# Layer 3 attention: a mixing laid out as two heads by two query halves, turned before the next scores

## The chip, the cores and the metric

The kernel runs on one core of one Trainium2 chip. The metric is the device time of one execution in microseconds, the median of the runs. The engines are named as the profile names them: PE multiplies matrices (PEld loads its stationary operands), DVE, ACT and POOL work on vectors, SP issues DMAs.

## The reference

The whole kernel is a decoder of four layers, each with an attention, a cross attention and a feed-forward block, on 16 times 128 = 2048 tokens of width 256. The change touches the attention of layer 3 alone:

```python
proj = jnp.einsum('bsd,ed->bse', x, proj_w) + proj_b
flat = jnp.transpose(proj.reshape(B, S, H, hd), (2, 0, 1, 3)).reshape(H, B * S, hd)
q = jnp.einsum('hnd,hde->hne', flat, wq)
k = jnp.einsum('hnd,hde->hne', flat, wk)
logits = jnp.einsum('hne,hme->hnm', q, k) / jnp.sqrt(jnp.asarray(D, x.dtype))
attn = jax.nn.softmax(logits, axis=-1)
out = jnp.einsum('hnm,hmd->hnd', attn, flat)
```

There are H = 16 heads of hd = 16, and all 2048 tokens attend to all 2048 in every head. The result is added to x.

## The kernel before, in words

`l3_attn` (from L4443) first projects and splits queries and keys into parts (phase "split"), and then runs the phase "heads", which is all that the change touches. It works in 32 units: eight pairs of heads by four chunks of 512 queries. A unit has 32 steps, sixteen tiles of 128 keys by two heads. The steps of all units are one sequence, `steps`, which every engine's program walks in the same order, starting 48 steps early (`LEAD`).

Each even step n has, in PE's own order (L4757 to L4771):

- two probes (L4727), queries against 512 keys, one per head of a pair. They run one unit and a half ahead and serve only to find each query's largest score; DVE takes the maximum of both in one reduction (L4783).
- `score(n)` (L4717), 128 keys by 512 queries of the first head, into one of three PSUM banks that rotate (`slot_of`, `SB` = 3). The row maxima are part of the operands, so ACT only has to take the exponential (L4820) into one of 16 `attn` tiles.
- half of `mix` (L4742), attention times values, for the scores of 8 steps ago. The values have 17 columns, 16 and a column of ones that gives the softmax sum, padded to 32. Four such strips stand side by side on the array: two heads by two key tiles. `mix(m, 0)` and `mix(m, 1)` do the two halves of 256 query columns.
- `score(n + 1)`, the second head. Both heads' operands have 50 rows, on different halves of the array (rows 0 to 49 and 64 to 113).

Each strip's product of one half is two recorded matmuls, so a half of `mix` shows eight. The strips add up in PSUM bank 7 (`mixed_bank`) over the unit's sixteen key tiles: 512 columns, and per head two partial sums, for even and odd key tiles.

When a unit has ended, its result is taken out during the next unit, at fixed steps (`ended_at`, L4658):

- step 6: ACT copies bank 7 to `output` (`out`, L4831, 128x512). The next unit's first `mix`, at step 8, waits for this copy (`outed`, L4738 to L4740), since it overwrites the bank.
- step 15, behind `score(15)`: PE turns `output` by four 128x128 transposes (`unturn`, L4752) into one of the three rotating banks; ACT copies that to `unturned` (`take`, L4837, 128x512), behind `exp(15)`.
- step 17: POOL adds the even and the odd partial sums (`add_halves`, L4893).
- step 24: DVE takes the reciprocal of the sums (`divide`, L4800); POOL multiplies (L4899) and adds to x (L4903).

POOL also rounds and lays the maxima into the queries for the unit after (`lay_rows`, L4885), and SP loads the next pair's operands.

Of the kernel before, what the change touches and what calls it, by code (L numbers as in the profile page):

```python
# [13 lines left out]
ALU = mybir.AluOpType  # L14
# [3 lines left out]
P = 128  # L18
# [7 lines left out]
PAD = 32  # L26
# [4416 lines left out]
def l3_attn(k):  # L4443
# [15 lines left out]
    with ExitStack() as stack:  # L4459
# [172 lines left out]
                    pool.wait_ge(s["lined"], 4)  # L4632

        RING, SPAN, LEAD = 16, 2 * QT, 48
        SB, PB = 3, 4
        UNITS = PAIRS * CHUNKS
        TOTAL = UNITS * SPAN
# [2 lines left out]
        peaks = sb(k, stack, "peaks", [P, 2, 4, 2, CHUNKS])  # L4640
        peak = sb(k, stack, "peak", [P, 2, 4, 2])
        peak_parts, peak_rows = (sb(k, stack, m, [P, 2, 4, 2, PAD]) for m in ("peak_parts", "peak_rows"))
        output = sb(k, stack, "output", [P, CHUNK])
        unturned = sb(k, stack, "unturned", [P, 4, 4, PAD])
        sums, fresh = sb(k, stack, "sums", [P, 4, 2, VW]), sb(k, stack, "fresh", [P, 4, 2, D])
        share = sb(k, stack, "share", [P, 4, 2])
        mixed_bank = k.ps[:, 7, :]
        steps = range(-LEAD, TOTAL + SPAN)
        OUT, UNTURN, SUM, DIVIDE, TURN, RAISE = 6, 15, 17, 24, 5, 8

        def scored(n):
            return 0 <= n < TOTAL
# [8 lines left out]

        slot_of = {}
        for n_ in steps:
            jobs = [("score", n_)] if scored(n_) else []
            if ended_at(n_, UNTURN) is not None:
                jobs.append(("unturn", ended_at(n_, UNTURN)))
            for job in jobs:
                slot_of[job] = len(slot_of)

        def bank(job):  # L4670
            return k.ps[:, slot_of[job] % SB, :]

        names = ("loaded0 loaded1 pool_step cleared fetched probed maxed peaked parted rows_turned raised scored read mixed outed "
                 "unturned summed shared added value_made value_took biased")
        with phase(k, "heads", names) as (block, s):
            loaded = [s[f"loaded{i}"] for i in range(2)]

# [15 lines left out]
            def _(pe):  # L4693
# [36 lines left out]
                        last.then_inc(s["probed"], 1)  # L4730

                def mix(m, half):
                    u, part = m // 8, m % 8
                    columns = sl(half, CHUNK // 2)
                    if half == 0:
                        pe.wait_ge(s["read"], slot_of["score", 4 * m + 3] + 1)
                    if part == 0 and half == 0:
                        pe.wait_ge(s["fetched"], u // CHUNKS + 1)  # L4738
                        if u >= 1:
                            pe.wait_ge(s["outed"], u)  # L4740
                    for strip in range(4):
                        last = nc.tensor.matmul(mixed_bank[sl(strip, PAD), columns], head_values[:, u // CHUNKS % 2, strip % 2, 2 * part + strip // 2, :],  # L4742
                                                attn[:, (4 * m + strip) % RING, columns], start=part == 0 and half == 0, stop=part == 7 and half == 1,
                                                skip_group_check=True)
                    if half == 1:
                        last.then_inc(s["mixed"], 1)

                def unturn(u):
                    pe.wait_ge(s["outed"], u + 1)
                    slot_free(("unturn", u))  # L4750
                    for b in range(4):
                        last = nc.tensor.transpose(bank(("unturn", u))[:, sl(b)], output[:, sl(b)], k.ident[:, :])  # L4752
                    last.then_inc(s["unturned"], 1)

# [2 lines left out]
                for n in steps:  # L4757
                    if n < 16 - LEAD and n % 4 == 0:
                        value(4 + (n + LEAD) // 4)
                    if n % 2 == 0:  # L4760
                        for p in (n + LEAD, n + LEAD + 1):
                            if p < TOTAL:
                                probe(p)
                        if scored(n):
                            score(n)
                        if scored(4 * (n // 4 - 2)):
                            mix(n // 4 - 2, n % 4 // 2)
                        if scored(n + 1):
                            score(n + 1)
                    if ended_at(n, UNTURN) is not None:  # L4770
                        unturn(ended_at(n, UNTURN))  # L4771

            @block.vector
            def _(dve):
                v = nc.vector
                v.memset(head_values[:, :, :, :, :], 0.0).then_inc(s["cleared"], 1)

                def peak_of(p):
                    r, i, at = p // SPAN, p % SPAN // 2, SB + p % PB
                    if i == 0 and r >= 2:  # L4780
                        dve.wait_ge(s["peaked"], r - 1)
                    dve.wait_ge(s["probed"], p // 2 + 1)
                    v.tensor_reduce(peaks[:, r % 2, i // CHUNKS, :, i % CHUNKS], k.ps[:, at:at + 2, :], AX.X, ALU.max).then_inc(s["maxed"], 1)  # L4783

                def peak_of_all(r):
                    dve.wait_ge(s["maxed"], 16 * (r + 1))
                    if r >= 2:
                        dve.wait_ge(s["parted"], r - 1)
                    v.tensor_reduce(peak[:, r % 2, :, :], peaks[:, r % 2, :, :, :], AX.X, ALU.max, negate=True).then_inc(s["peaked"], 1)  # L4789

                def turn_rows(r):
                    dve.wait_ge(s["parted"], r + 1)
                    if r >= 2:
                        dve.wait_ge(s["raised"], 8 * (r - 1))
                    v.transpose(peak_rows[:, r % 2, :, :, :].rearrange("p b a c -> p (b a c)"),  # L4795
                                peak_parts[:, r % 2, :, :, :].rearrange("p b a c -> p (b a c)")).then_inc(s["rows_turned"], 1)

                def divide(u):
                    dve.wait_ge(s["summed"], u + 1)
                    v.reciprocal(share[:, :, :].unsqueeze(3), sums[:, :, :, D:VW]).then_inc(s["shared"], 1)  # L4800

                for n in steps:
                    p = n + LEAD
                    if p < TOTAL:
                        if p % 2:
                            peak_of(p - 1)
                        if p % SPAN == SPAN - 1:
                            peak_of_all(p // SPAN)
                    if row_at(n, TURN) is not None:
                        turn_rows(row_at(n, TURN))  # L4810
                    if ended_at(n, DIVIDE) is not None:
                        divide(ended_at(n, DIVIDE))

            @block.scalar
            def _(act):
# [17 lines left out]
                def take(u):  # L4833
                    act.wait_ge(s["unturned"], u + 1)
                    if u >= 1:
                        act.wait_ge(s["summed"], u)
                    nc.scalar.activation(unturned[:, :, :, :].rearrange("p b a w -> p (b a w)"), bank(("unturn", u)),  # L4837
                                         ACT.Copy).then_inc(s["read"], 1)

                for i in range(QT // 2):  # L4840
                    take_values(i)
                for n in steps:
                    if scored(n):
                        exp(n)
                    if ended_at(n, OUT) is not None:
                        out(ended_at(n, OUT))
                    if ended_at(n, UNTURN) is not None:
                        take(ended_at(n, UNTURN))

            @block.gpsimd  # L4850
            def _(pool):
                link = Link(pool, s["pool_step"])
                g_ = nc.gpsimd
                done = {"fetched": 0, "parted": 0, "summed": 0, "added": 0}

                def fetch(pair):
                    if pair == 0:
# [27 lines left out]
                            g_.tensor_copy(rows[:, :, quarter, :], peak_rows[PAD * quarter:PAD * quarter + 2, r % 2, :, a, :]).then_inc(s["raised"], 1)  # L4885
                    pool.wait_ge(s["raised"], 8 * (r + 1))

                def add_halves(u):
                    pool.wait_ge(s["read"], slot_of["unturn", u] + 1)
                    if u >= 1:  # L4890
                        pool.wait_ge(s["shared"], u)
                        pool.wait_ge(s["added"], 2 * u)
                    g_.tensor_tensor(sums[:, :, :, :], unturned[:, :, 0:2, 0:VW], unturned[:, :, 2:4, 0:VW], ALU.add).then_inc(s["summed"], 1)  # L4893
                    done["summed"] += 1

                def add(u):
                    pair, c = u // CHUNKS, u % CHUNKS
                    pool.wait_ge(s["shared"], u + 1)
                    g_.tensor_tensor(fresh[:, :, :, :], sums[:, :, :, 0:D], share[:, :, :].unsqueeze(3).broadcast_to([P, 4, 2, D]),  # L4899
                                     ALU.mult).then_inc(s["added"], 1)  # L4900
                    pool.wait_ge(s["added"], 2 * u + 1)
                    x = k.x[:, sl(c, 4), sl(pair, 2 * D)].rearrange("p b (a d) -> p b a d", a=2)
                    g_.tensor_tensor(x, x, fresh[:, :, :, :], ALU.add).then_inc(s["added"], 1)  # L4903
                    done["added"] += 2

                def add_bias(i):
# [11 lines left out]
                for n in steps:  # L4918
# [3 lines left out]
                        lay_rows(row_at(n, RAISE))  # L4922
                    if n > 0 and n % (CHUNKS * SPAN) == CHUNKS * SPAN - 16 and n // (CHUNKS * SPAN) + 1 < PAIRS:
                        fetch(n // (CHUNKS * SPAN) + 1)
                    if ended_at(n, SUM) is not None:
                        add_halves(ended_at(n, SUM))
                    if ended_at(n, DIVIDE) is not None:
                        add(ended_at(n, DIVIDE))

# [222 lines left out]
```

## Time and profile before

| | us |
|---|---|
| runs | 3328.42, 3354.23, 3327.92 |
| median | 3328.42 |
| span of the profiled execution, first to last instruction | 3397.0 |
| of it, phase "heads": first probe to the end of the last addition to x | 2429.4 to 3148.1 |

The profile knows no other time of that execution than its span. Times inside it are counted from the span's start.

### The profile page before, as it was taken

What the parts mean: (1) busy time and instruction counts of PE and PEld (TensorE: products, weight loads), DVE (VectorE), ACT (ScalarE), POOL (GpSimd) and SP (SyncE); (2) the same over time, 40 slices, a digit from 0 to 9 for tenths busy, and PEclk for the clock granted to TensorE, in tenths of its full rate; (3) what the DMA queues carried; (4) which work ended last, traced back from release to release, by engine and by line L of the source; (5) the groups of instructions that cost most, each with busy time, mean ns of one, the idle gap of its engine ahead of it and who ended that gap; (6) DMA issues with size and microseconds to landing.
All of it is one profiled execution on the core that took longest, in us unless ns stands there. A gap on an engine that the chain in (4) does not pass through costs nothing. (4 is left out here: it accounts for less than half of the span.)

```text
span 3397.0 us, 59298 instructions
## 1 busy us (share of the span) xinstructions
PE 3009.1 (89%) x20925; PEld 1857.6 (55%) x20929; DVE 2235.3 (66%) x4489; ACT 1822.0 (54%) x4182; POOL 1132.7 (33%) x1288
## 2 busy tenths in 40 slices
PE   7979759998887799987799989797799999999889
PEld 4656548877664556653467657454333333333567
DVE  6777645454546656667567747525589999996672
ACT  6967713333213344445566645211278888888554
POOL 3535555433432022215166653012111111221333
PEclk9999869999998999998889999898789999999989
DMA  9300156665530000022000032132401111110300
GB/s 301 133 9 2 47 203 210 207 188 173 158 101 26 26 1 1 1 73 85 33 1 1 1 118 106 64 109 88 113 1 20 20 21 20 21 20 1 125 13 25
DMA packets 158228, 243.61 MB, mean 72 GB/s; under 512 B 21298, under 2 KB 130482, under 8 KB 152482
## 3 DMA queue, kind: packets, MB, share of 16 engines
q1 hardware_dynamic: 144114, 202.05, 19.6%
q0 software_dynamic: 13824, 37.77, 3.4%
q8 instruction: 173, 2.83, 0.4%
q14 instruction: 117, 0.96, 0.1%
HBM read 132.64 MB, written 107.10 MB: 71 GB/s over the span
## 5 line engine op out<-in xcount | busy, mean ns | idle before, releaser
L4783 DVE TENSOR_REDUCE peaks<-ps 128x2 f32<-128x1024 f32 x512 | 617.6, 1219 | 64.8 <-PE ps L4727 63.0
L4820 ACT ACTIVATE attn<-ps 128x512 f32<-128x512 f32 x1024 | 558.8, 596 | 113.1 <-PE ps L4717 56.8
L4717 PE MATMUL ps<-queries,keys 50*128 50x512 f32 x1024 | 383.8, 455 | 0.0
L4727 PE MATMUL ps<-keys,queries 50*128 50x512 f32 x1024 | 370.2, 468 | 12.8 <-DVE peaks L4783 7.9
L4742 PE MATMUL ps<-attn,head_values 128*32 128x256 f32 x4096 | 332.3, 397 | 9.2 <-ACT output L4831 9.2
L4717 PEld LDWEIGHTS ps<-queries,keys 50*128 50x128 f32 x1024 | 157.6, 188 | 215.6 <-ACT attn L4820 197.5
L1239 POOL TENSOR_TENSOR attn_w<-attn_w,attn_share 128x512 f32<-128x512 f32 x128 | 131.7, 1050 | 373.0 <-DVE attn_share L1085 373.0
L2133 PE MATMUL ps<-experts,tileT 128*128 x884 | 232.0, 385 | 2.1 <-issue 2.1
L2340 DVE COPY normed<-ps 128x256 f32<-128x256 f32 x221 | 93.8, 424 | 202.9 <-PE ps L2149 106.8
L4742 PEld LDWEIGHTS ps<-attn,head_values 128*32 128x32 f32 x4096 | 82.3, 108 | 197.9 <-issue 108.6
L2194 ACT ACTIVATE tileT<-ps 128x256 f32<-128x256 f32 x221 | 84.6, 383 | 168.4 <-PE ps L2117 115.7
L2149 PE MATMUL ps<-experts,hiddenT 128*128 (+1 forms) x474 | 147.2, 392 | 25.1 <-DVE hiddenT L2349 21.1
L2133 PEld LDWEIGHTS ps<-experts,tileT 128*128 128x128 f32 x884 | 153.2, 193 | 19.4 <-issue 3.8
L4727 PEld LDWEIGHTS ps<-keys,queries 50*128 50x128 f32 x1024 | 147.5, 192 | 28.4 <-DVE peaks L4783 16.6
L2200 ACT ACTIVATE gate<-ps 128x128 f32<-128x128 f32 x237 | 65.8, 277 | 173.9 <-PE ps L2133 152.6
L1076 DVE TENSOR_REDUCE attn_peak<-ps 128x4 f32<-128x512 f32 x128 | 87.7, 685 | 95.9 <-PE ps L958 95.9
L4870 POOL CAST peak_parts<-peak 128x8 fp32r<-128x8 f32 x32 | 6.3, 197 | 407.4 <-DVE peak L4789 387.8
L2050 POOL DMA_INDIRECT rows<-expert_rows,index x96 | 91.0, 948 | 150.2 <-DMA expert_rows<-normed 60.9
L972 PE MATMUL ps<-xT,L_xattn_Wq 128*128 128x512 f32 x256 | 124.7, 610 | 7.7 <-ACT qT L1176 6.2
L2038 POOL DMA_INDIRECT routed_rows<-rows,index x96 | 96.3, 1003 | 87.7 <-DVE normed L2340 61.5
L2149 PEld LDWEIGHTS ps<-experts,hiddenT 128*128 128x128 f32 x474 | 86.8, 191 | 52.8 <-issue 41.1
L4885 POOL CAST queries<-peak_rows 2x128 fp32r<-2x128 f32 x256 | 73.5, 287 | 125.3 <-DVE peak_rows L4795 111.6
(733 smaller groups left out, 7164.5 us busy)
## 6 DMA issues: line engine op xcount, KB each, us to landing
tile_in<-routed_rows SPq DMA_DIRECT2D x244, 128.0 KB, 2.2
expert_rows<-normed SPq DMA_DIRECT2D x221, 128.0 KB
routed_rows<-zeros SPq DMA_DIRECT2D x2, 8064.0 KB, 48.1
experts<-in_L_ffn_experts SPq DMA_DIRECT2D x4, 3072.0 KB
routed_rows<-zeros SPq DMA_DIRECT2D x1, 12160.0 KB, 67.0
kT<-L_xattn_keys SPq DMA_DIRECT2D x8, 1024.0 KB
v<-L_xattn_values SPq DMA_DIRECT2D x8, 1024.0 KB, 8.7
experts<-in_L_ffn_experts SPq DMA_DIRECT2D x8, 1024.0 KB
```

Of the source, the lines that this page charges most:

```text
L972: last = nc.tensor.matmul(query_bank, wq[:, kt, sl(4 * p + jj)], xT[g % 2][:, kt, :], start=kt == 0, stop=kt == KD - 1)
L1239: nc.gpsimd.tensor_tensor(w, w, share[:, n % 2, side, :].unsqueeze(2).broadcast_to([P, 4, P]), ALU.mult).then_inc(s_["scaled"], 1)
L2038: nc.gpsimd.indirect_dma_start(rows_dram[g][:, :], bass.IndirectOffsetOnAxis(index_of(slice(t, t + 1))[:, 0, c:c + 1], 0), rows[:, t, :], ...
L2050: nc.gpsimd.indirect_dma_start(rows[:, TOP * (t % 2) + c, :], None, back_dram[g][:, :], bass.IndirectOffsetOnAxis(index[:, t, c:c + 1], 0) ...
L2133: last = nc.tensor.matmul(gate_bank(u), x, weight(u, 2 * kt * INNER, 2 * INNER), start=False, stop=kt == KD - 1)
L2149: nc.tensor.matmul(out_bank(u), hiddenT[:, u % 2, :], weight(u, 2 * KD * INNER, DIM), start=is_tile(u), stop=True).then_inc(s["downed"], 1)
L2340: v.tensor_copy(tile_out[:, u % 4, :], out_bank(u)).then_inc(s["out_taken"], 1)
L4717: nc.tensor.matmul(bank(("score", n)), keys[pair % 2][rows, sl(kt)], queries[pair % 2][rows, sl(c, CHUNK)], start=True, stop=True).then_in ...
L4727: last = nc.tensor.matmul(k.ps[:, SB + p % PB, :], queries[pair % 2][rows, sl(t)], keys[pair % 2][rows, sl(c, CHUNK)], start=True, stop=True)
L4742: last = nc.tensor.matmul(mixed_bank[sl(strip, PAD), columns], head_values[:, u // CHUNKS % 2, strip % 2, 2 * part + strip // 2, :], attn[ ...
L4783: v.tensor_reduce(peaks[:, r % 2, i // CHUNKS, :, i % CHUNKS], k.ps[:, at:at + 2, :], AX.X, ALU.max).then_inc(s["maxed"], 1)
L4820: nc.scalar.activation(attn[:, n % RING, :], bank(("score", n)), ACT.Exp, scale=1.0 / 16.0).then_inc(s["read"], 1)
```

## The change

The four strips of `mix` become two heads by two halves of the query columns. `mix(m, half)` now does one key tile for all 512 queries, where it did two key tiles for half of them: `block` is the key tile, `side` the query half. So no strip is a partial sum, the result is 256 columns instead of 512, and `add_halves` with its semaphore goes. `out` and `take` copy 256 columns, `unturn` has two transposes. POOL's last addition is two instructions of half the size, as the blocks now lie two tiles apart in x.

`unturn` moves from behind `score(15)` to in front of it, directly behind the `mix` of step 14; its bank stands before that of `score(15)` in the rotation, and ACT's `take` moves in front of `exp(15)`. `mix` waits for its exponentials in both halves, each time for the two tiles that it reads. `divide`, `take` and `add` wait for other semaphores in place of the removed one.

```diff
@@ -4632,6 +4632,7 @@
         RING, SPAN, LEAD = 16, 2 * QT, 48
+        HALF = CHUNK // 2
         SB, PB = 3, 4
@@ -4640,13 +4641,12 @@
-        output = sb(k, stack, "output", [P, CHUNK])
-        unturned = sb(k, stack, "unturned", [P, 4, 4, PAD])
-        sums, fresh = sb(k, stack, "sums", [P, 4, 2, VW]), sb(k, stack, "fresh", [P, 4, 2, D])
-        share = sb(k, stack, "share", [P, 4, 2])
-        mixed_bank = k.ps[:, 7, :]
+        output = sb(k, stack, "output", [P, HALF])
+        unturned, fresh = sb(k, stack, "unturned", [P, 2, 4, PAD]), sb(k, stack, "fresh", [P, 2, 4, D])
+        share = sb(k, stack, "share", [P, 2, 4])
+        mixed_bank = k.ps[:, 7, 0:HALF]
         steps = range(-LEAD, TOTAL + SPAN)
-        OUT, UNTURN, SUM, DIVIDE, TURN, RAISE = 6, 15, 17, 24, 5, 8
+        OUT, UNTURN, DIVIDE, TURN, RAISE = 6, 15, 24, 5, 8
@@ -4661,9 +4661,9 @@
-            jobs = [("score", n_)] if scored(n_) else []
-            if ended_at(n_, UNTURN) is not None:
-                jobs.append(("unturn", ended_at(n_, UNTURN)))
+            jobs = [("unturn", ended_at(n_, UNTURN))] if ended_at(n_, UNTURN) is not None else []
+            if scored(n_):
+                jobs.append(("score", n_))
@@ -4730,17 +4730,16 @@
                 def mix(m, half):
-                    u, part = m // 8, m % 8
-                    columns = sl(half, CHUNK // 2)
-                    if half == 0:
-                        pe.wait_ge(s["read"], slot_of["score", 4 * m + 3] + 1)
-                    if part == 0 and half == 0:
+                    u, block = m // 8, 2 * (m % 8) + half
+                    pe.wait_ge(s["read"], slot_of["score", 4 * m + 2 * half + 1] + 1)
+                    if block == 0:
                         pe.wait_ge(s["fetched"], u // CHUNKS + 1)
                         if u >= 1:
                             pe.wait_ge(s["outed"], u)
                     for strip in range(4):
-                        last = nc.tensor.matmul(mixed_bank[sl(strip, PAD), columns], head_values[:, u // CHUNKS % 2, strip % 2, 2 * part + strip // 2, :],
-                                                attn[:, (4 * m + strip) % RING, columns], start=part == 0 and half == 0, stop=part == 7 and half == 1,
+                        side, a = strip // 2, strip % 2
+                        last = nc.tensor.matmul(mixed_bank[sl(strip, PAD), :], head_values[:, u // CHUNKS % 2, a, block, :],
+                                                attn[:, (4 * m + 2 * half + a) % RING, sl(side, HALF)], start=block == 0, stop=block == QT - 1,
                                                 skip_group_check=True)
@@ -4748,7 +4747,7 @@
                 def unturn(u):
-                    for b in range(4):
+                    for b in range(2):
@@ -4765,10 +4764,10 @@
                             mix(n // 4 - 2, n % 4 // 2)
+                        if ended_at(n + 1, UNTURN) is not None:
+                            unturn(ended_at(n + 1, UNTURN))
                         if scored(n + 1):
                             score(n + 1)
-                    if ended_at(n, UNTURN) is not None:
-                        unturn(ended_at(n, UNTURN))
@@ -4796,8 +4795,10 @@
                 def divide(u):
-                    dve.wait_ge(s["summed"], u + 1)
-                    v.reciprocal(share[:, :, :].unsqueeze(3), sums[:, :, :, D:VW]).then_inc(s["shared"], 1)
+                    dve.wait_ge(s["read"], slot_of["unturn", u] + 1)
+                    if u >= 1:
+                        dve.wait_ge(s["added"], 2 * u)
+                    v.reciprocal(share[:, :, :].unsqueeze(3), unturned[:, :, :, D:VW]).then_inc(s["shared"], 1)
@@ -4833,25 +4834,25 @@
                 def take(u):
                     act.wait_ge(s["unturned"], u + 1)
                     if u >= 1:
-                        act.wait_ge(s["summed"], u)
-                    nc.scalar.activation(unturned[:, :, :, :].rearrange("p b a w -> p (b a w)"), bank(("unturn", u)),
+                        act.wait_ge(s["added"], 2 * u)
+                    nc.scalar.activation(unturned[:, :, :, :].rearrange("p b c w -> p (b c w)"), bank(("unturn", u))[:, 0:HALF],
                                          ACT.Copy).then_inc(s["read"], 1)
                 for n in steps:
+                    if ended_at(n, UNTURN) is not None:
+                        take(ended_at(n, UNTURN))
                     if scored(n):
                         exp(n)
                     if ended_at(n, OUT) is not None:
                         out(ended_at(n, OUT))
-                    if ended_at(n, UNTURN) is not None:
-                        take(ended_at(n, UNTURN))
@@ -4885,22 +4886,18 @@
-                def add_halves(u):
...
-                    g_.tensor_tensor(sums[:, :, :, :], unturned[:, :, 0:2, 0:VW], unturned[:, :, 2:4, 0:VW], ALU.add).then_inc(s["summed"], 1)
...
                 def add(u):
                     pair, c = u // CHUNKS, u % CHUNKS
                     pool.wait_ge(s["shared"], u + 1)
-                    g_.tensor_tensor(fresh[:, :, :, :], sums[:, :, :, 0:D], share[:, :, :].unsqueeze(3).broadcast_to([P, 4, 2, D]),
+                    if u >= 1:
+                        pool.wait_ge(s["added"], 2 * u)
+                    g_.tensor_tensor(fresh[:, :, :, :], unturned[:, :, :, 0:D], share[:, :, :].unsqueeze(3).broadcast_to([P, 2, 4, D]),
                                      ALU.mult).then_inc(s["added"], 1)
                     pool.wait_ge(s["added"], 2 * u + 1)
-                    x = k.x[:, sl(c, 4), sl(pair, 2 * D)].rearrange("p b (a d) -> p b a d", a=2)
-                    g_.tensor_tensor(x, x, fresh[:, :, :, :], ALU.add).then_inc(s["added"], 1)
+                    for b in range(2):
+                        x = k.x[:, 4 * c + b:4 * c + b + 3:2, sl(pair, 2 * D)].rearrange("p s (a d) -> p s a d", a=2)
+                        last = g_.tensor_tensor(x, x, fresh[:, b, :, :].rearrange("p (s a) d -> p s a d", s=2), ALU.add)
+                    last.then_inc(s["added"], 1)
@@ -4922,8 +4919,6 @@
-                    if ended_at(n, SUM) is not None:
-                        add_halves(ended_at(n, SUM))
```

## Rows read from the trace of the kernel before

**Rows 1.** The page, its head and part 1: busy us, share, instructions.

```profile
span 3397.0 us, 59298 instructions
...
PE 3009.1 (89%) x20925; PEld 1857.6 (55%) x20929; DVE 2235.3 (66%) x4489; ACT 1822.0 (54%) x4182; POOL 1132.7 (33%) x1288
```

**Rows 2.** Busy time by stretch: stretch, length, PE, PEld, DVE, ACT, POOL, clock, DMA.

```profile
2661.00:2761.00 100.00, 98.57 (x932) 37.53 (x930) 93.74 (x91) 87.53 (x162) 17.81 (x57) 1.00 0.12 17
...
2707.77:2728.86 21.09, 20.80 (x198) 7.91 (x198) 19.82 (x20) 18.45 (x36) 4.61 (x14) 1.00 0.20 33
```

**Rows 3.** Waits, 2480 to 3110 us: waiter, released by, us, times, longest.

```profile
DVE peaks L4783 <- PE ps L4727: 40.3, 94, 1.0
...
PE ps L4742 <- ACT output L4831: 8.6, 30, 0.3
```

**Rows 4.** Timeline of PE, steps 5 to 9: start, busy us, instruction.

```profile
2706.27 0.50 PE L4717 MATMUL ps<-queries,keys 50*128 50x512 f32 x1
...
2706.93 0.64 PE L4742 MATMUL ps<-attn,head_values 128*32 128x256 f32 x8
...
2707.50 0.50 PE L4717 MATMUL ps<-queries,keys 50*128 50x512 f32 x1
...
2707.84 0.39 PE L4717 MATMUL ps<-queries,keys 50*128 50x512 f32 x1
...
2708.52 0.64 PE L4742 MATMUL ps<-attn,head_values 128*32 128x256 f32 x8 [0.29 <-ACT output L4831]
...
2709.09 0.49 PE L4717 MATMUL ps<-queries,keys 50*128 50x512 f32 x1
```

**Rows 5.** Timeline of PE, the mixing of step 14 to step 17.

```profile
2712.22 0.64 PE L4742 MATMUL ps<-attn,head_values 128*32 128x256 f32 x8
...
2712.79 0.49 PE L4717 MATMUL ps<-queries,keys 50*128 50x512 f32 x1
...
2713.21 0.66 PE L4752 MATMUL ps<-ident,output 128*128 128x128 f32 x4
...
2713.79 0.50 PE L4727 MATMUL ps<-keys,queries 50*128 50x512 f32 x2
...
2714.45 0.64 PE L4742 MATMUL ps<-attn,head_values 128*32 128x256 f32 x8
...
2715.02 0.49 PE L4717 MATMUL ps<-queries,keys 50*128 50x512 f32 x1
```

**Rows 6.** Timeline of PE, the first three of those four transposes.

```profile
2713.21 0.55 PE L4752 MATMUL ps<-ident,output 128*128 128x128 f32 x3
```

**Rows 7.** Timeline of ACT over the same steps.

```profile
2707.77 0.60 ACT L4831 ACTIVATE output<-ps 128x512 f32<-128x512 f32 x1
...
2708.25 1.11 ACT L4820 ACTIVATE attn<-ps 128x512 f32<-128x512 f32 x2
...
2713.90 0.60 ACT L4837 ACTIVATE unturned<-ps 128x512 f32<-128x512 f32 x1
```

**Rows 8.** The page, part 5: ACT copying 256 columns out of PSUM.

```profile
L2194 ACT ACTIVATE tileT<-ps 128x256 f32<-128x256 f32 x221 | 84.6, 383 | 168.4 <-PE ps L2117 115.7
```

**Rows 9.** Timeline of DVE: after the transposes, and three reductions after a delay.

```profile
2714.41 1.23 DVE L4783 TENSOR_REDUCE peaks<-ps 128x2 f32<-128x1024 f32 x1 [0.64 <-PE ps L4727]
...
2719.73 3.45 DVE L4783 TENSOR_REDUCE peaks<-ps 128x2 f32<-128x1024 f32 x3
```

**Rows 10.** Timeline of ACT in the last unit, which has no probes.

```profile
3133.49 0.60 ACT L4837 ACTIVATE unturned<-ps 128x512 f32<-128x512 f32 x1
...
3134.91 8.12 ACT L4820 ACTIVATE attn<-ps 128x512 f32<-128x512 f32 x15 [0.34 <-PE ps L4717]
```

**Rows 11.** Timeline at the end of the stage.

```profile
3146.35 0.47 POOL L4893 TENSOR_TENSOR sums<-unturned 128x136 f32<-128x136 f32 x1 [10.45 <-ACT unturned L4837]
...
3146.85 0.20 DVE L4800 RECIPROCAL share<-sums 128x8 f32<-128x8 f32 x1 [11.97 <-POOL sums L4893]
...
3147.62 0.45 POOL L4903 TENSOR_TENSOR x<-x,fresh 128x128 f32<-128x128 f32 x1
```

More of the change, by code:

```diff
@@ L4673, in l3_attn @@
         names = ("loaded0 loaded1 pool_step cleared fetched probed maxed peaked parted rows_turned raised scored read mixed outed "
-                 "unturned summed shared added value_made value_took biased")
+                 "unturned shared added value_made value_took biased")
         with phase(k, "heads", names) as (block, s):
@@ L4853, in _ @@
                 g_ = nc.gpsimd
-                done = {"fetched": 0, "parted": 0, "summed": 0, "added": 0}
+                done = {"fetched": 0, "parted": 0, "added": 0}
                 def fetch(pair):
@@ L4886, in lay_rows @@
                     pool.wait_ge(s["raised"], 8 * (r + 1))
-                def add_halves(u):
[L4889 to L4892, printed above, removed]
-                    g_.tensor_tensor(sums[:, :, :, :], unturned[:, :, 0:2, 0:VW], unturned[:, :, 2:4, 0:VW], ALU.add).then_inc(s["summed"], 1)
-                    done["summed"] += 1
                 def add(u):
```

## Prediction

> **What bounds the kernel now.** I read the page's head first: PE is the busiest engine, but 89% over a whole program of many stages decides nothing [rows 1]. So I went to the busy time by stretch. In the stage of the change PE is busy for 98.6 of 100 us at a granted clock of 1.00, DVE for 93.7, ACT for 87.5 [rows 2]. The waits say which of the three leads. DVE idles for PE's probes, 40.3 us in 94 waits, and PE waits for ACT's copy of the result 30 times, once a unit, 8.6 us in all [rows 3]. The timeline of PE shows why. Without an event, a pair of steps takes from score to score 2707.50 - 2706.27 = 1.23 us: 0.66 up to the mixing, in which four products go in two waves (two run side by side on different halves of the array, so 0.33 a wave), and 0.57 for the mixing [rows 4]. No gap is left in it. PE sets the pace and DVE follows.
>
> Two events of each unit break it. At step 8 the mixing waits for the copy: 2709.09 - 2707.50 = 1.59, so 0.36 more [rows 4]. At step 15 the result is turned: 2715.02 - 2712.79 = 2.23, so 1.00 more [rows 5]. Fourteen pairs of 1.23 and these two make 21.04; the unit takes 21.09 [rows 2], so nothing is missing but rounding. DVE's idle time behind the turn is 0.64 [rows 9], the turn again.
>
> **Step 1, the copy.** ACT's copy takes 0.60 for 512 columns [rows 7]. The nearest row for 256 columns out of PSUM has a mean of 383 ns [rows 8], so 0.22 less. The copy starts at 2707.77 in any case, behind the exponential before it [rows 7], and the mixing starts at 2708.52, 0.15 after the copy's end [rows 4, 7]. With 0.22 less a wait of 0.14 is left of the 0.36. Bounds: nothing, if the start of the copy decides and the length doesn't, and all of 0.36. I take 0.22, since the mixing follows the end of the copy directly. There are 30 such waits [rows 3]: 6.6 us.
>
> **Step 2, the turn.** The 1.00 has two parts. From 2712.79 to 2713.21 `score(15)` runs alone, 0.42 [rows 5]; elsewhere it shares its wave with a probe. From 2713.21 to 2713.79 four transposes take 0.58, and from there to the mixing it is 0.66 as ever, so the three products left fill two waves anyway [rows 5]. In the new place score, probes and score stay together, and the 0.42 goes whole. Of the 0.58 two transposes go: three are busy for 0.55, four for 0.66 [rows 5, 6], so one is 0.11 and 0.58 - 0.22 = 0.36 stays. That saves 0.64. The trace shows no mixing followed by a transpose. Its price above a mixing followed by a score lies between 0 and 0.10: a lone score followed by the transposes took 0.42 where a wave takes 0.33 [rows 4, 5]. I take 0.05, the middle, as neither row is nearer, and 0.59 a turn. The probes end 48 steps before the scores, which is step 975, where the turn of the thirtieth unit stands: 29 turns have probes behind them, 29 x 0.59 = 17.1 us.
>
> The rule that speaks against this step is in the Trainium skill, page "TensorEngine Tiling (Array Packing)", section "Key Properties": a change of the tiling mode, not merely of the tile, drains the array. The turn as it stands lies between two products on array halves, the new one between four column strips and array halves. By the rule the new entry drains too and the price is the whole 0.10, 1.5 us less gain in all; by the row of mixing to score, which changes the mode within its 0.57, it would be 0 and 1.5 us more. The 0.42 agrees that some such change costs something.
>
> **What the moved turn holds up.** Behind it on PE stand `score(15)`, two probes and `score(16)`. It waits for the copy of step 8, which ended some 5 us before [rows 5, 7], and for a bank that ACT read three scores back. On ACT `take` now stands before `exp(15)`. The last transposition ends about 0.8 after the mixing's second half began, the copy takes 0.38, and `exp(15)` has its scores 1.2 after the same moment (0.36 + 0.33 for the turn, 0.49 for the score [rows 4 to 6]), so the copy is over about when the scores arrive. If that cover fails, ACT has 18.45 of 21.09 [rows 2], less 0.43 for two shorter copies, and catches up within a few pairs: 0 to 0.2 a unit; I take 0.
>
> **Step 3, everything else in the loop.** The mixing has as many products of the same 256 columns. Its waits ask for exponentials that ended more than a pair of steps earlier; a wait there was before, in every second mixing, and the pairs are alike. POOL loses the 0.47 of `sums` [rows 11] and gains one addition; it is busy for 4.61 of 21.09 [rows 2], and `lay_rows`, its only work that PE waits for, keeps its place. DVE's reciprocal waits for ACT's copy, long done by step 24. SP keeps its program. All this is hidden at 0; it would cost 0.1 a unit at most if POOL's second addition came in front of `lay_rows`, which it doesn't in program order.
>
> Next late after this: DVE is busy for 19.82 of a unit [rows 2], and the new unit is 21.09 - 0.22 - 0.59 = 20.28. That leaves room, more than it looks: when their data wait, three reductions take 3.45 [rows 9], 1.15 each where the busy time counts 1.23.
>
> **Step 4, the end.** In the last unit and a half ACT leads: 15 exponentials in 8.12, 0.54 each; a turn costs it 3134.91 - 3133.49 - 0.54 = 0.88, of which 0.34 is idle [rows 10]. Two turns there save 0.2 to 0.5 each, one copy 0.2 to 0.4. After the last mixing everything stands in a row: the copy (0.22), two transposes (0.22), `take` (0.22), `sums` to reciprocal (3146.85 - 3146.35 = 0.50) go, and the second addition comes in, between 0 and the 0.45 of the whole one [rows 11], say 0.2. That is 1.0. In all 2.0, bounds 1.3 and 2.8.
>
> **Sum.** 6.6 + 17.1 + 2.0 = 25.7 us. The profiled execution's span is 3397.0 [rows 1], 2% over the median of the runs, 3328.42; that the profile gives no other time of it leaves open where the 69 us lie. The stage ran at full clock and its pairs are alike, so I take the saving in microseconds as it is: 3397.0 - 25.7 = 3371.3 in a profile, 3328.4 - 25.7 = 3302.7, so 3303 as the median. That is 0.8%; about 1% is what a measurement of this kernel can tell from no change, so the likeliest outcome counts as none.
>
> **Rivals.**
>
> - Both events nearly vanish. The wait for the copy goes whole (0.36) and only the 0.22 of two transposes stays of the 1.00. For it: 0.58 for four transposes is more than 4 x 0.11, and the rest could be the change between array halves and whole array, which might hide behind the mixing as it does for the scores. Against: a copy of 0.38 behind 2707.77 ends at 2708.15, when the mixing would be due at about 2708.17 (2707.84 + 0.33), and the signal took 0.15 [rows 4, 7]. 30 x 0.36 + 29 x 0.78 + 2.8 = 36.2: 3292.
> - The turn costs a fixed amount. The 1.00 is the price of leaving and entering the whole array and only the 0.22 goes. For it: the lone score's 0.42 is more than a wave. Against: 0.33 of the 0.42 is that wave itself, which has a partner again. 6.6 + 29 x 0.22 + 1.3 = 14.3: 3314.
> - Slower: the strips collide. Two strips of a mixing now read the same `attn` tile at two column offsets, and two have the same stationary operand; in the trace of before the four strips read four tiles. If reads of one tile exclude each other, each mixing of 0.57 [rows 4] grows, sixteen times a unit; from 0.81 / 16 = 0.05 a mixing, 9%, the gain is gone. Run in series it would be 0.57 more: 32 x 16 x 0.57 = 292, 3594. For it speaks only that no row shows such reads; against it, that the eight products of a half start as a group in every mixing, whatever they read.
> - The change does not reach its place: the copy or the turn is held by ACT, and only one of the two gains comes. That lies between the second rival and the forecast.
>
> **How the numbers follow.** Forecast, with the last case between, 0.66; nearly vanishing 0.15; fixed amount 0.13; collision 0.06. The forecast's own bounds are 3297 to 3310 (the price of the entry 0 to 0.10, the copy 0.1 to 0.3, the end 1.3 to 2.8, and 0.1 a unit for ACT). The range takes in the second case and the third, and some spread of the runs (two of the three lie 0.5 apart, one 26 above): 3289 to 3320. Faster by over 1% means below 3295: most of the second case and a little of the first, 0.16. Slower by over 1% is the collision, 0.05. The rest, 0.79, is within 1%.
>
> **What would show it.** In the changed profile: copies of about 0.38 on both lines; a wait of the mixing for the copy of 0.1 to 0.2; the transposes in pairs, directly behind a mixing, 0.36 to the next score; `score(15)` beside a probe again; pairs of 1.23 as before; a unit of about 20.28. A pair of steps other than 1.23 would make the prediction wrong from the ground, a turn that still costs over 0.8 the second step, and DVE without idle time would mean that it leads.

## The result, and the profile after

The changed kernel takes 3310.6 us in the median of nine runs, the kernel before, run beside it, 3333.0. The ratio is 0.9928, 95% interval 0.9911 to 0.9946. At 3333 that is 24 us less, where the two medians lie 22.3 apart. 25.7 were forecast, and the forecast of 3303 was made against a median of 3328.4. The gain is below the 1% that had been named as no change, but the interval does not reach 1. In a second series of runs the ratio was 0.9904, interval 0.9881 to 0.9926, or 32 us less.

The profiled execution of the changed kernel spans 3315.8 us, where that of the kernel before spans 3397.0 [rows 1]. These 81 us are mostly not the change's: the first probe starts at 2429.4 in the one trace and at 2377.8 in the other, so 52 us lie in stages ahead of it that have the same code. The change is read from its own stage.

Busy time by stretch, the changed kernel, one unit and 100 us (columns as in [rows 2]):

```profile
2644.82:2665.06 20.24, 20.17 (x196) 7.51 (x196) 19.78 (x20) 17.92 (x36) 4.31 (x14) 1.00 0.22 34
2640.00:2740.00 100.00, 99.64 (x962) 37.09 (x958) 97.69 (x95) 88.53 (x168) 19.75 (x67) 1.00 0.12 18
```

A unit takes 20.24 us instead of 21.09, and all 29 from the first copy to the thirtieth are alike. PE is busy for 99.6% of the time instead of 98.6, DVE for 97.7 instead of 93.7.

Timeline of PE, the changed kernel, the mixing of step 8 that waits for the copy and then the turn behind the mixing of step 14 (answers to [rows 4] and [rows 5]):

```profile
2663.55 0.50 PE L4717 MATMUL ps<-queries,keys 50*128 50x512 f32 x1
...
2664.78 0.50 PE L4717 MATMUL ps<-queries,keys 50*128 50x512 f32 x1
...
2665.13 0.39 PE L4717 MATMUL ps<-queries,keys 50*128 50x512 f32 x1
2665.59 0.64 PE L4741 MATMUL ps<-attn,head_values 128*32 128x256 f32 x8
2666.16 0.49 PE L4717 MATMUL ps<-queries,keys 50*128 50x512 f32 x1
...
2669.29 0.64 PE L4741 MATMUL ps<-attn,head_values 128*32 128x256 f32 x8
2669.86 0.44 PE L4751 MATMUL ps<-ident,output 128*128 128x128 f32 x2
2670.23 0.49 PE L4717 MATMUL ps<-queries,keys 50*128 50x512 f32 x1
2670.23 0.72 PE L4727 MATMUL ps<-keys,queries 50*128 50x512 f32 x2
```

A pair without an event still takes 2664.78 - 2663.55 = 1.23. With the copy it takes 2666.16 - 2664.78 = 1.38, so 0.15 more instead of 0.36. The turn comes 0.57 after its mixing's start (2669.86 - 2669.29), just where a score would, and the next score 0.37 later, beside a probe: the turn costs 0.37 instead of 1.00.

Timeline of ACT, the same unit (answers to [rows 7]):

```profile
2665.06 0.39 ACT L4832 ACTIVATE output<-ps 128x256 f32<-128x256 f32 x1
2665.32 1.11 ACT L4821 ACTIVATE attn<-ps 128x512 f32<-128x512 f32 x2
2666.69 3.55 ACT L4821 ACTIVATE attn<-ps 128x512 f32<-128x512 f32 x6 [0.26 <-PE ps L4717]
2670.34 0.38 ACT L4838 ACTIVATE unturned<-ps 128x256 f32<-128x256 f32 x1
2670.76 3.55 ACT L4821 ACTIVATE attn<-ps 128x512 f32<-128x512 f32 x6
```

The copies last 0.39 and 0.38 instead of 0.60. The second one ends at 2670.72, and `exp(15)` follows at 2670.76, without idle time between.

DVE's idle time behind its small reduction of the maxima, and the end of the stage (answers to [rows 9] and [rows 11]), the changed kernel:

```profile
2671.06 3.62 DVE L4782 TENSOR_REDUCE peaks<-ps 128x2 f32<-128x1024 f32 x3 [0.22 <-PE ps L4727]
```

```profile
3064.89 0.38 ACT L4838 ACTIVATE unturned<-ps 128x256 f32<-128x256 f32 x1 [0.53 <-PE ps L4751]
3065.31 0.20 DVE L4801 RECIPROCAL share<-unturned 128x8 f32<-128x8 f32 x1 [11.82 <-ACT unturned L4838]
3065.59 0.40 POOL L4894 TENSOR_TENSOR fresh<-unturned,share 128x128 f32<-128x128 f32 x1 [10.95 <-DVE share L4801]
3066.07 0.59 POOL L4899 TENSOR_TENSOR x<-x,fresh 128x64 f32<-128x64 f32 x2
```

DVE waits 0.22 for PE there, instead of 0.64. At the end the reciprocal comes 0.42 after the start of ACT's copy, with nothing between; the two additions take 0.59 instead of 0.45.

Where the gain came from: 29 units of 0.85 are 24.6 us, and from the thirtieth copy to the end of the stage it is 37.3 us instead of 39.65, another 2.4. These 27 us are the same in both traces of the change. The stretch from the first probe to the first copy differs too, 67.5 before and 64.6 after, and is taken up in the last section.

### The profile page after: what moved, and what is told of

Its sections match the earlier page's. It is cut to its first block and busy times, and to the rows that moved or that the text cites. A ratio compares the mean times of both kernels' runs of the same rounds, so it can differ in the third digit from the quotient of the medians.

```text
span 3315.8 us, 59147 instructions
## 1 busy us (share of the span) xinstructions
PE 2973.0 (90%) x20865; PEld 1843.2 (56%) x20865; DVE 2232.8 (67%) x4489; ACT 1809.1 (55%) x4182; POOL 1123.5 (34%) x1288
## 5 line engine op out<-in xcount | busy, mean ns | idle before, releaser
L2117 PE MATMUL ps<-ident,tile_in 128*128 128x128 f32 x442 | 85.6, 276 | 31.3 <-DMA tile_in<-routed_rows 20.4
```

## The experiments

All edits are against the changed kernel or the kernel before, as said. Unit lengths are the distances of ACT's copies of the result in one profile; there are 29 in each, alike to within 0.04.

**The place alone.** The kernel before, with its layout, copies and partial sums, and the turn moved:

```diff
+                        if ended_at(n + 1, UNTURN) is not None:
+                            unturn(ended_at(n + 1, UNTURN))
                         if scored(n + 1):
                             score(n + 1)
-                    if ended_at(n, UNTURN) is not None:
-                        unturn(ended_at(n, UNTURN))
```

(and `take` in front of `exp(15)`, with its slot). Expected:

> The layout, the copies and the partial sums of before, but the turn of four transposes directly behind the mixing of step 14, and the copy after it ahead of exp(15). My theory (the place gives back the lone score, the transposes cost 0.11 each wherever they stand): the event of the turn goes from 1.00 to 0.58 us, the unit from 21.09 to 20.67, 29 turns give about 12 us, ratio to before 0.996. Rival, a fixed price of entering and leaving the whole array: the event stays near 1.00, the unit at 21.09, ratio 1.000.

Measured: ratio to before 0.9955, interval 0.9941 to 0.9969; a unit of 20.67. Timeline of PE:

```profile
2638.22 0.64 PE L4742 MATMUL ps<-attn,head_values 128*32 128x256 f32 x8
2638.79 0.66 PE L4752 MATMUL ps<-ident,output 128*128 128x128 f32 x4
2639.37 0.50 PE L4717 MATMUL ps<-queries,keys 50*128 50x512 f32 x1
2639.38 0.73 PE L4727 MATMUL ps<-keys,queries 50*128 50x512 f32 x2
```

The four transposes take 0.58, as they did in their old place [rows 5], and nothing else is left of the 1.00: the mixing and the score beside a probe follow as in any other pair. The rival of a fixed price falls.

**The layout alone.** The changed kernel with the turn and its copy back behind `score(15)` and `exp(15)` (the edit above, reversed). Expected:

> The new layout with copies of 256 columns and two transposes, but the turn stays behind score(15), and its copy behind exp(15). My theory: 0.21 less at the copy and 0.22 less at the turn, the lone score of 0.42 stays, the unit goes from 21.09 to 20.66, some 13 us and 1 to 2 at the end, ratio 0.9955. Rival, the fixed price: the same here, and the unit of the full change would then be 20.66 too, which it isn't; so this run and the one of the place alone must add up to the full change, 0.42 and 0.43 of 0.85.

Measured: ratio 0.9957, interval 0.9942 to 0.9971; a unit of 20.65. Timeline of PE:

```profile
2851.32 0.49 PE L4717 MATMUL ps<-queries,keys 50*128 50x512 f32 x1
2851.75 0.44 PE L4751 MATMUL ps<-ident,output 128*128 128x128 f32 x2
2852.11 0.50 PE L4727 MATMUL ps<-keys,queries 50*128 50x512 f32 x2
```

Two transposes, 0.36; but `score(15)` is alone again for 0.43. The two halves of the change give 0.42 and 0.44 a unit, from lengths rounded to 0.01, and the whole gives 0.85: they add up and don't overlap. The end of the stage splits as well. From the thirtieth copy to the end it is 39.65 us before, 39.17 with the place alone, 37.76 with the layout alone and 37.29 with both, so the layout gives 1.9 of the 2.4 and the place 0.5.

**Two more transposes.** The changed kernel with

```diff
-                    for b in range(2):
-                        last = nc.tensor.transpose(bank(("unturn", u))[:, sl(b)], output[:, sl(b)], k.ident[:, :])
+                    for b in (2, 3, 0, 1):
+                        last = nc.tensor.transpose(bank(("unturn", u))[:, sl(b)], output[:, sl(b % 2)], k.ident[:, :])
```

Expected:

> The changed kernel with two more transposes in each turn, of the same blocks, into the unused half of the bank. My theory: 0.11 each, the unit goes from 20.24 to 20.46, so the number of transposes counts. Rival, the fixed price: 20.24, only the change of array layout counts.

Measured (this kernel and the next ran once, so only the lengths within their profiles are compared): a unit of 20.46, as the count of transposes has it, 0.11 each. Timeline of PE:

```profile
2642.76 0.66 PE L4751 MATMUL ps<-ident,output 128*128 128x128 f32 x4
2643.35 0.50 PE L4717 MATMUL ps<-queries,keys 50*128 50x512 f32 x1
```

**ACT's order.** The changed kernel with `take` behind `exp(15)`; PE's order is unchanged, and the bank of the turn stands behind that of `score(15)` in the rotation again. Of the edit, ACT's part:

```diff
-                    if ended_at(n, UNTURN) is not None:
-                        take(ended_at(n, UNTURN))
                     if scored(n):
                         exp(n)
                     if ended_at(n, OUT) is not None:
                         out(ended_at(n, OUT))
+                    if ended_at(n, UNTURN) is not None:
+                        take(ended_at(n, UNTURN))
```

Expected:

> The changed kernel with ACT's copy of the turned block behind exp(15) again, and the slots in that order. My theory: ACT is no limit and the order of the two doesn't matter, the unit stays at 20.24 within 0.05. Rival, ACT's order is part of the gain: exp(15) first makes the copy late, the score that takes over its bank waits, and the unit grows by 0.2 to 0.4.

Measured: a unit of 20.25. Timeline of ACT:

```profile
2639.88 0.60 ACT L4821 ACTIVATE attn<-ps 128x512 f32<-128x512 f32 x1 [0.53 <-PE ps L4717]
2640.38 0.38 ACT L4838 ACTIVATE unturned<-ps 128x256 f32<-128x256 f32 x1
```

ACT now idles for 0.53 ahead of `exp(15)`, and it costs 0.01 a unit. The step that hid the move of `take` at nothing is right: ACT has that much to spare in the 29 units. At the end of the stage, where ACT leads, it has not: from the thirtieth copy to the last addition it is 3018.98 to 3056.89, 37.9 instead of 37.3. There the order is worth 0.6.

**The copy first.** What is left of the copy's wait is 0.15. The changed kernel with `out` in front of `exp(6)`:

```diff
+                    if ended_at(n, OUT) is not None:
+                        out(ended_at(n, OUT))
                     if scored(n):
                         exp(n)
-                    if ended_at(n, OUT) is not None:
-                        out(ended_at(n, OUT))
```

Expected of it, and of the changed kernel once more beside it:

> The changed kernel with ACT's copy of the result in front of exp(6) instead of behind it. My theory (the next unit's mixing follows the end of this copy, and the copy starts late only because an exponential stands before it): the copy starts about 0.1 us earlier in the unit, the wait of the mixing falls from 0.14 to about 0.04, the unit goes from 20.24 to about 20.14, 3 us in all. Rival: the exponentials now behind the copy hold up score(9), whose bank exp(6) frees, and the unit stays at 20.24 or grows.

> The changed kernel once more, beside the one with the copy first. Every theory: a unit of 20.24 us, and a ratio to before of 0.993 within 0.002; the time from the first probe to the first copy may differ, since the granted clock was not alike there in the profiles so far.

Measured: a unit of 20.18, and 20.24 for the changed kernel beside it; ratios to before 0.9899, interval 0.9871 to 0.9926, and 0.9904, interval 0.9881 to 0.9926. So the changed kernel's unit came out as expected and its ratio did not: 0.9904 lies just below the 0.991 to 0.995 that were named, though its interval reaches into them. Timelines of ACT and of PE, the copy first:

```profile
2627.02 0.39 ACT L4832 ACTIVATE output<-ps 128x256 f32<-128x256 f32 x1 [0.24 <-PE ps L4741]
2627.30 4.98 ACT L4821 ACTIVATE attn<-ps 128x512 f32<-128x512 f32 x9
```

```profile
2626.89 0.50 PE L4717 MATMUL ps<-queries,keys 50*128 50x512 f32 x1
...
2627.55 0.64 PE L4741 MATMUL ps<-attn,head_values 128*32 128x256 f32 x8
2628.12 0.50 PE L4717 MATMUL ps<-queries,keys 50*128 50x512 f32 x1
2628.12 0.73 PE L4727 MATMUL ps<-keys,queries 50*128 50x512 f32 x2
2628.47 0.47 PE L4717 MATMUL ps<-queries,keys 50*128 50x512 f32 x1
2628.86 0.64 PE L4741 MATMUL ps<-attn,head_values 128*32 128x256 f32 x8
```

Both sides were half right. The copy starts 0.13 behind the first score of its pair instead of 0.28. It no longer waits for an exponential, but 0.24 for PE's mixing, the last of its unit. The wait of the next mixing is gone altogether: that pair takes 2628.12 - 2626.89 = 1.23. But in the next pair it is 0.74 from the first score to the mixing, where it was 2627.55 - 2626.89 = 0.66, and its second score lasts 0.47. That is `score(10)`, whose bank `exp(7)` frees, and ACT now runs nine exponentials without a gap behind the copy. The timeline of PEld for the same two pairs, and ACT's `exp(6)` and `exp(7)`, show what held it:

```profile
2626.88 0.18 PEld L4717 LDWEIGHTS ps<-queries,keys 50*128 50x128 f32 x1 [0.41 <-ACT attn L4821]
...
2627.00 0.19 PEld L4717 LDWEIGHTS ps<-queries,keys 50*128 50x128 f32 x1
...
2628.12 0.18 PEld L4717 LDWEIGHTS ps<-queries,keys 50*128 50x128 f32 x1 [0.41 <-ACT attn L4821]
...
2628.43 0.18 PEld L4717 LDWEIGHTS ps<-queries,keys 50*128 50x128 f32 x1
```

```profile
2627.30 1.08 ACT L4821 ACTIVATE attn<-ps 128x512 f32<-128x512 f32 x2
```

The load of `score(10)`'s operands starts 0.31 behind the first load of its pair, where in the pair before it is 0.12, and 0.05 after `exp(7)` ends at 2628.38; it is 0.05 in every unit of this trace. The program has this score wait for `exp(7)`, so by the times it was the bank that held it up; no kernel was run with more banks. 0.06 a unit is 1.8 us in all; the two ratios don't tell these kernels apart, the unit lengths do.

## Why the prediction was right

What bounds the stage, and that DVE and ACT only follow: held. The pair of 1.23 stayed the same through every variant that left it alone, with either layout of the strips, so the collision of reads is excluded, too.

Step 1, the copy: 0.21 a unit against the forecast 0.22 (0.36 to 0.15). The guess that the mixing follows the copy's end, not its start, was right: the copy starts 0.28 behind its pair's score where it was 0.27, the mixing starts 0.14 behind the copy's end where it was 0.15, and only the length between has changed. The copy first shows the rest: where the copy starts early enough, too, the wait vanishes. The rival in which the wait goes whole needed that; the change alone leaves 0.15 of it, and 0.37 of the turn instead of that rival's 0.22.

Step 2, the turn: 0.63 against 0.59. The two parts were as reckoned, the lone score (0.42, by the place alone) and two transposes of 0.11. The allowance of 0.05 for a mixing followed by a transpose was the one thing too much: the first transpose comes 0.57 after the mixing's start, exactly as a score does. The upper end of 0.10 had been read from the lone score's 0.42 against 0.33 for a wave. That row doesn't tell of transposes. In the stretch without probes two scores go in one wave and a mixing follows, and there, too, it takes 0.44 (3118.05 - 3117.61; timeline of PE, the kernel before):

```profile
3117.61 0.51 PE L4717 MATMUL ps<-queries,keys 50*128 50x512 f32 x2
3118.05 0.64 PE L4742 MATMUL ps<-attn,head_values 128*32 128x256 f32 x8
```

So a wave of scores that stands alone costs 0.42 to 0.44 before transposes and before a mixing alike, and two waves in a row cost 0.66: by these rows the second adds 0.66 - 0.44 = 0.22. That is why the lone score was dear in its old place; in the new one it fills a half of a wave that stood empty. In either case another kind of product follows, so it stays open how much of the 0.42 is a price of the change of kind. The drain of which the Trainium skill speaks ("TensorEngine Tiling (Array Packing)", "Key Properties") is not to be seen between the column strips and the transposes, where the time is the same 0.57 as to a score; the run doesn't show whether it hides in the 0.57.

Steps 3 and 4: POOL, SP and the new waits cost nothing that shows in a unit of 20.24 against the forecast 20.28. `take` was over when its neighbour's scores arrived, as forecast: the copy ends at 2670.72, and so does `score(15)` (2670.23 + 0.49). From the thirtieth copy on it was 2.4, of which 0.21 is that copy's, so the end gave 2.2 against 2.0; the second addition cost 0.14 of the 0.2 allowed.

The sum of these is 27 against 25.7. The measured 24 us, with an interval from 18 to 30 (0.0054 and 0.0089 of 3333), agrees with both, and so do the 32 us of the second series, interval 25 to 40. The runs alone could not have told the mechanism; the pairs and units do. A slip of the sums changes nothing: the forecast's own bounds, added up from the terms that it lists, are some 3298 to 3311 and not 3297 to 3310. The span was no guide to the median: the executions of the two traces differ by 52 us ahead of the stage.

## What to carry to other kernels

When two products run side by side on halves of the array, a third thing put between them can cost its own time and that of the one left alone, here 0.58 and 0.42: place it where the kind of product changes anyway, as between a mixing and the next scores. Length and place of such an event were separate gains here and could be reckoned separately, each from one timeline of the engine that never idles. A copy that the leading engine waits for can be shortened or started earlier; the second moves the delay to the work queued behind it, so half of what it gained here came back one pair later.

## What had not been expected

The start of the stage goes by the granted clock and not by the kernel. From the first probe to the first copy it took 67.5 us in the trace before and 64.6 in that after, but 59.8 with the place alone and 62.4 with the changed kernel once more, the same code. Busy time from the first probe to the first copy: the kernel before, the changed kernel, the place alone, the copy first (the clock is the third number from the end):

```profile
2429.45:2496.91 67.46, 59.56 (x281) 25.01 (x283) 52.15 (x48) 24.19 (x44) 10.14 (x25) 0.61 0.14 18
```

```profile
2377.79:2442.42 64.63, 56.64 (x281) 24.20 (x283) 52.15 (x48) 24.20 (x44) 10.14 (x25) 0.64 0.14 19
```

```profile
2367.29:2427.04 59.75, 51.83 (x281) 22.85 (x283) 51.83 (x48) 24.19 (x44) 10.14 (x25) 0.70 0.16 21
```

```profile
2365.49:2425.22 59.73, 51.84 (x281) 22.80 (x283) 51.67 (x48) 23.82 (x42) 10.15 (x25) 0.70 0.15 20
```

The place alone has the layout of before and the copy first that of after; at the same mean clock of 0.70 they take the same time. So the 3 us by which the trace after is ahead here go with its clock, 0.64 against 0.61, and not with the change. Busy time of 10 us, the kernel before, and then the place alone:

```profile
2480.00:2490.00 10.00, 10.00 (x60) 3.48 (x60) 5.68 (x7) 4.89 (x10) 2.30 (x8) 0.50 0.00 0
```

```profile
2407.80:2417.80 10.00, 10.00 (x78) 3.41 (x80) 7.69 (x8) 6.70 (x13) 1.25 (x5) 0.74 0.00 2
```

Before, PE was still at 0.50 (1.2 GHz) 51 to 61 us after the first probe; with the place alone it had risen to 2.4 GHz in part of the stretch 41 to 51 us after it. PE was busy throughout both. Why it rises earlier in one execution than in another stays open, and with it how much of the spread of the runs it makes.
